# Eleven projections of the last layer's chunks: one f32 product in four passes, or three products of rounded parts

## The reference, cut to what matters

```python
xn = rmsnorm(h) * g_sio                      # h: layer norm of x, scaled and shifted
z  = sigmoid(xn @ w_ln_z.T + b_ln_z)         # in logs in the reference
dt = xn @ w_dt.T + b_dt
h_t = sigmoid(-dt) * h_{t-1} + z * sigmoid(dt)     # a scan over each sequence
y  = (h_t @ w_y.T + b_y) * silu(xn @ w_yact.T + b_yact)
x1 = h + y
xn2 = rmsnorm(x1) * g_ffn
hid = (xn2 @ w_fc.T + b_fc) * silu(xn2 @ w_fcact.T + b_fcact)   # 128 -> 512 features
x2 = x1 + hid @ w_out.T + b_out
# then x = x + gate * x2, a layer norm, and a channel mix: three 128x128 products
```

## Time and profile before

| | us |
|---|---|
| median of three runs (lowest to highest) | 768.26 (766.97 to 769.05) |
| the profiled execution | 762.66 |
| its span, first to last instruction | 760.9 |
| TensorE busy in the span | 696.3 |
| VectorE, ScalarE, GpSimd busy | 505.9, 481.8, 388.6 |

### The profile page before, as it was taken

One profiled execution on the slowest core, in us unless ns is written; L12 is line 12 of the kernel. 1 busy time (PEld: TensorE's weight loads), 2 busy tenths in 40 slices (PEclk: granted clock), 3 DMA queues, 4 the chain that ended last, 5 costly groups with the idle time before them and its releaser, 6 DMA issues.

```text
span 760.9 us, 12350 instructions
## 1 busy us (share of the span) xinstructions
PE 696.3 (92%) x3608; PEld 424.0 (56%) x3608; DVE 505.9 (66%) x1906; ACT 481.8 (63%) x734; POOL 388.6 (51%) x562
## 2 busy tenths in 40 slices
PE   4999999999997999887999699996999999999994
PEld 4544444545444544347988699984655544444442
DVE  2598879989998899973452244422345678795572
ACT  2767687677784767565544355552587959777553
POOL 7427354656776667742422255534455575722253
PEclk9999999999999999998999899999899999999998
DMA  9992000000000000028676688811010101000002
GB/s 273 380 383 70 1 1 0 9 15 15 19 19 16 14 15 22 22 84 236 193 203 206 192 249 245 243 51 32 28 29 24 33 23 40 25 4 0 0 15 83
DMA packets 65597, 66.79 MB, mean 88 GB/s; under 512 B 7105, under 2 KB 48410, under 8 KB 65530
## 3 DMA queue, kind: packets, MB, share of 16 engines
q1 hardware_dynamic: 59152, 52.46, 22.8%
q0 software_dynamic: 6320, 13.53, 5.6%
q10 hardware_dynamic: 58, 0.02, 0.0%
HBM read 37.80 MB, written 28.18 MB: 87 GB/s over the span
## 4 chain that ended last, share of the span: by engine, by line
PE 56%; DVE 22%; issue 7%; ACT 5%; DMA 4%; SPq 2%; POOL 2%; DVEq 0%; ACTq 0%; POOLq 0%
PE PS L1085 9%; DVE JK L1271 8%; PE PS L948 4%; PE PS L1135 3%; PE PS L891 3%; PE PS L986 3%; PE PS L1066 3%; PE PS L1149 3%; PE PS L1142 3%; PE PS L897 2%; PE PS L903 2%; PE PS L988 2%; PE PS L911 1%; DMA got<-expert_out,IG 1%; PE PS L1072 1%
## 5 line engine op out<-in xcount | busy, mean ns | idle before, releaser
L1271 DVE CUSTOM_DVE_ANT_0 JK<-PS,CM 128x256 bf16<-128x256 f32 (+1 forms) x512 | 149.1, 351 | 7.0 <-PE PS L948 5.7
L1763 ACT ACTIVATE GF<-PS,XN 128x256 f32<-128x256 f32 x156 | 73.5, 475 | 72.9 <-PE PS L1074 41.6
L948 PE MATMUL PS<-KZ,QS 128*128 128x512 f32 x192 | 88.4, 497 | 7.8 <-DVE MX L1271 5.6
L1085 PE MATMUL PS<-WD,GF 128*128 128x128 f32 x624 | 94.0, 276 | 0.0
L1941 POOL DMA_INDIRECT got<-expert_out,IG x64 | 64.5, 1007 | 50.3 <-DMA got<-expert_out,IG 33.1
L1085 PEld LDWEIGHTS PS<-WD,GF 128*128 128x128 f32 x624 | 86.4, 193 | 2.8
L1913 POOL DMA_INDIRECT expert_rows<-five,IU x64 | 63.3, 990 | 32.5 <-DMA expert_rows<-five,IU 14.9
L1724 ACT ACTIVATE PA<-PS 128x1024 f32<-128x1024 f32 x64 | 64.7, 1026 | 15.2 <-PE PS L971 14.1
L1863 POOL TENSOR_SCALAR H<-xc,MOD 128x256 f32<-128x256 f32 x56 | 33.3, 603 | 68.0 <-DVE xc L1240 60.8
L1900 POOL TENSOR_SCALAR_AFFINE_SELECT PA<-PA 128x256 f32<-128x256 f32 x128 | 49.8, 419 | 27.9 <-ACT PA L1724 27.3
L1924 POOL DMA_DIRECT2D expert_out<-YT x39 | 21.7, 558 | 80.3 <-DVE YT L1523 80.3
(11 more groups left out here) (289 smaller groups left out, 1710.1 us busy)
## 6 DMA issues: line engine op xcount, KB each, us to landing
expert_rows<-five SPq DMA_DIRECT2D x16, 1024.0 KB, 12.6
WU<-in_L_ffn_up_w SPq DMA_DIRECT2D x39, 256.0 KB, 3.2
WD<-in_L_ffn_down_w SPq DMA_DIRECT2D x39, 256.0 KB, 3.4
XT<-expert_rows SPq DMA_DIRECT2D x39, 128.0 KB, 3.7
expert_out<-YT POOLq DMA_DIRECT2D x39, 128.0 KB, 3.4
BD<-in_L_ffn_down_b SPq DMA_DIRECT2D x39, 64.0 KB, 3.3
PA<-in_L_attn_x SPq DMA_DIRECT2D x8, 256.0 KB, 5.5
out<-yo SPq DMA_DIRECT2D x8, 256.0 KB, 2.4
```

The lines of the kernel that those rows point to most:

```text
L948: pe.matmul(bk.rearrange("p (j n) -> p j n", n=wd), q, ks, start=True, stop=True).then_inc(sems["mx_mm"], 1)
L1085: m = pe.matmul(bk[:, b], g[:, b], wd[:, k, :], start=(k == 0 and t == 0), stop=(k == 3 and t == blocks - 1))
L1271: m = dve.tensor_tensor_reduce(JK[n % 2][:, s], bk[:, s], CM[:, 256 - wd:256] if wd == 128 else CM[:, 0:256], -1.0, 3.0e38, ALU.add, ALU.m ...
L1763: act.activation(GF[slot["gf", kind, u, k]][:, 0:n], bank("up", kind, u, k)[:, 0:n], ACT.Gelu, bias=bias).then_inc(sems["gelu"], 1)
```

## The change

The 88 products of normed rows are made from rounded parts. `rmsnorm` for the norms "g" and "h" now writes its f32 result over the reciprocal roots (the `rs` buffers) instead of XN; a new ACT stage `xhi` copies it to a float32r tile `xh`, a new POOL stage `xlo` writes the difference to `xl` (three pairs of such tiles); each product becomes three float32r matmuls, high weight by high rows, low weight by high rows and high weight by low rows. `zd` does the four matmuls with high rows first and then waits for the low ones. The weights' parts are made once in the experts' stage by three new DVE subtractions (`twl`). The product of low by low is not computed.

Around it: the first sigmoid factor A goes to XN instead of a ring of its own; the output copies have two buffers instead of three, `rr` two instead of three; the weights are turned in five groups instead of six. `ORDER2` is written anew, `ORDER1` gets the three `twl` steps. Two entries in `NARROW`, the table of how long TensorE is really active in a stage, change what `arrange` believes of attention, so that it places fillers at new points: 17 groups of fillers instead of 7, mostly of one matmul. Gathers wait for each other as before.

```diff
+PARTS = (0, 2, 3)
...
-NARROW = {"dpm": 0.06, "rtm": 0.05, "vm": 0.15, "modmm": 0.2}
+NARROW = {"dpm": 0.06, "rtm": 0.05, "vm": 0.15, "modmm": 0.2, "atm": 0.11, "mxm": 0.213}
...
-LANDS = {"gather": 2.5, "scatter": 2.5, "fetch": 3.0}
+LANDS = {"gather": 2.5, "scatter": 2.5, "fetch": 3.0, "store": 2.0}
...
-    "APAPAAAAAAAAAPAPAPAPACACACACAAAAAAAAAAAAAAAAAEAEAEAEAAAAAAAAAAAAAAAAAGAGAGAAAAAPAXAXAXAAAAADAPAPABAAAIAPAGAIAPAPAPAPAAAA"
...
+    "APAPAPAAAAAAAPACACAAAAAAAAAAAEAEACACAAAAAAAAAAAAAAAAAEAEAXAXAXAAAAAAAAABAPAPAPAGAGAGAGAAAPAPAAAPAPAPAPAPAPAIAAAAAAAAAAAP"
...
-        yield stage("rms_rs", c, s, takes=[(RS_, "rrs", (c, s), ("xn", c, s))])
+        yield stage("rms_rs", c, s, takes=[(RS_, "rrs", (c, s), ("xn" if s == "q" else "xl", c, s))])
         yield stage("rms_norm", c, s, after=[("vecs",)])
+        if s != "q":
+            yield stage("xhi", c, s, takes=[(XP, "xp", (c, s), ("ya_mm", c) if s == "g" else ("f_mm", c, 3))])
+            yield stage("xlo", c, s)
 
...
-        for n in range(6):
-            yield stage("tw", n, takes=[(RR, "tw", (n,), ("tw_hi", n))], after=[("up", "s", NS - 1, 3), ("load_late",)])
+        for n in range(5):
+            yield stage("tw", n, takes=[(RR, "tw", (n,), ("tw_lo" if n in PARTS else "tw_hi", n))], after=[("up", "s", NS - 1, 3), ("load_late",)])
+            if n in PARTS:
+                yield stage("twl", n)
...
-        yield stage("rec", c, takes=[(SZ, "sz", (c,), ("Bz", c)), (SD, "sd", (c,), ("Bz", c)), (AA, "A", (c,), ("hs", c))])
+        yield stage("rec", c, takes=[(SZ, "sz", (c,), ("Bz", c)), (SD, "sd", (c,), ("Bz", c))])
...
-        yield stage("yam", c, takes=[(BK, "ya_bk", (c,), ("ya", c))], after=[("rms_norm", c, "g")])
+        yield stage("yam", c, takes=[(BK, "ya_bk", (c,), ("ya", c))], after=[("zd", c)])
...
-        yield stage("fam", c, k, takes=[(BK, "fa_bk", (c, k), ("fa", c, k))], after=[("rms_norm", c, "h")])
+        yield stage("fam", c, k, takes=[(BK, "fa_bk", (c, k), ("fa", c, k))], after=[("xhi", c, "h"), ("xlo", c, "h")])
-        yield stage("fm", c, k, takes=[(BK, "f_bk", (c, k), ("hf", c, k))])
+        yield stage("fm", c, k, takes=[(BK, "f_bk", (c, k), ("hf", c, k))], after=[("fm", c, k - 1)] if k else [])
...
-        yield stage("yo", c, takes=[(YO, "yo", (c,), ("yo", c))])
+        yield stage("yo", c, takes=[(YO, "yo", (c,), ("store", c))])
...
-TURN = ((0, 2), (2, 4), (6, 1), (7, 4), (11, 4), (15, 4))
-NAMES = ["L1_attn_w_ln_z", "L1_attn_w_dt", "L1_attn_w_y", "L1_attn_w_yact", "L1_ffn_W_r", "L1_ffn_W_k", "L1_ffn_W_v"]
+TURN = ((0, 3), (3, 4), (7, 4), (11, 4), (15, 4))
+NAMES = ["L1_attn_w_ln_z", "L1_attn_w_dt", "L1_attn_w_yact", "L1_attn_w_y", "L1_ffn_W_r", "L1_ffn_W_k", "L1_ffn_W_v"]
...
-    WL = sb("WL", [128, 19, 128])
+    WL, WLH, WLO = sb("WL", [128, 8, 128]), sb("WLH", [128, 11, 128], R), sb("WLO", [128, 11, 128], R)
...
+    xh, xl = ([sb(f"{n}{k}", [128, CH], R) for k in range(3)] for n in ("xh", "xl"))
...
+    def parts(k):
+        k = k if k < 3 else k - 4
+        return WLH[:, k, :], WLO[:, k, :]
...
-            pe.matmul(bank("z", c), wl["L1_attn_w_ln_z"], chunk(XN, c), start=True, stop=True).then_inc(sems["z_mm"], 1)
-            for e in prior["d", c]:
-                w.wait_ge(*at(*e))
-            pe.matmul(bank("d", c), wl["L1_attn_w_dt"], chunk(XN, c), start=True, stop=True).then_inc(sems["d_mm"], 1)
+            high, low = rounded(c, "g")
+            w.wait_ge(*at("xh", c, "g"))
+            w.wait_ge(*at("tw_lo", 0))
+            for use, k in (("z", 0), ("d", 1)):
+                for e in prior[use, c]:
+                    w.wait_ge(*at(*e))
+                pe.matmul(bank(use, c), parts(k)[0], high, start=True, stop=False)
+                pe.matmul(bank(use, c), parts(k)[1], high, start=False, stop=False)
+            w.wait_ge(*at("xl", c, "g"))
+            pe.matmul(bank("z", c), parts(0)[0], low, start=False, stop=True).then_inc(sems["z_mm"], 1)
+            pe.matmul(bank("d", c), parts(1)[0], low, start=False, stop=True).then_inc(sems["d_mm"], 1)
 
...
+            pe.matmul(bank("fa_bk", c, k), parts(11 + k)[0], high, start=True, stop=False)
+            pe.matmul(bank("fa_bk", c, k), parts(11 + k)[1], high, start=False, stop=False)
+            pe.matmul(bank("fa_bk", c, k), parts(11 + k)[0], low, start=False, stop=True).then_inc(sems["fa_mm"], 1)
...
-            if s == "h":
-                w.wait_ge(*at("ya_mm", c))
-            dve.scalar_tensor_tensor(two(chunk(XN, c)), hc(c), weight, two(rs_of("rrs", c, s)), ALU.mult, ALU.mult
-                                     ).then_inc(sems["xn"], 1)
+            o = chunk(XN, c) if s == "q" else rs_of("rrs", c, s)
+        def twl(n):
+            k0, kn = TURN[n]
+            o = k0 if k0 < 3 else k0 - 4
+            w.wait_ge(*at("tw_hi", n))
+            dve.tensor_tensor(WLO[:, o:o + kn, :].rearrange("p k d -> p (k d)"), bank("tw", n)[:, 0:128 * kn],
+                              WLH[:, o:o + kn, :].rearrange("p k d -> p (k d)").bitcast(F), ALU.subtract).then_inc(sems["tw_lo"], 1)
...
-            A, Bv = aa[slot["A", c]], bz[slot["Bz", c]]
+            A, Bv = chunk(XN, c), bz[slot["Bz", c]]
...
+        def xhi(c, s):
+            w.wait_ge(*at("xn", c, s))
+            for e in prior["xp", c, s]:
+                w.wait_ge(*at(*e))
+            act.activation(rounded(c, s)[0], rs_of("rrs", c, s), ACT.Copy).then_inc(sems["xh"], 1)
...
+        def xlo_(c, s):
+            high, low = rounded(c, s)
+            w.wait_ge(*at("xh", c, s))
+            pool.tensor_tensor(low, rs_of("rrs", c, s), high.bitcast(F), ALU.subtract).then_inc(sems["xl"], 1)
```

120 lines of the change are left out of this document (64 added, 56 removed), and 5 rows, old and new, of tables (HELD, SIGNALS).

## The result

The changed kernel takes 778.59 us (median of four, 772.06 to 782.07) beside 768.65 for the kernel before: a ratio of 1.0101, with a 95% interval from 1.0058 to 1.0145. With two later batches of runs it was timed 22 times, with a median of 777.0; the kernel before, timed beside every batch of later runs, 92 times, with 768.2. So it is slower by about 1.1%, where 763.3 and faster had been forecast, with a range of 754 to 771. The 92 runs of before lie between 761.4 and 774.9 us, 1.8% and not the 0.3% of the first three. A ratio takes only runs within 1.5% of the fastest of their kernel; medians are over all runs.

The account below looks back on a forecast made before the run. Gathers and VectorE, together with TensorE, bound the last layer until chunk 7's `fin2` (673.9 us), TensorE's work after it. Terms -6.0 + 0 + 0 + 1.0 + 0 = -5.0 us took the median from 768.26 to 763.3, range 754 to 771.

Parts of the forecast that it names:

- The price of a pass: TensorE's 88 changed products: 0.23 us per single pass, three cost 0.69 instead of 0.86, so each saves 0.17.
- what it saves behind the hinge: From chunk 7's `fin2` to the end: TensorE's remaining work falls from 74.5 to 68.5 us, saving 6.0.
- the hinge: Start of chunk 7's `fin2`, 673.9 us: gathers and VectorE decide ahead of it together with TensorE, TensorE's remaining work behind it.
- Ahead of the hinge 0: First to last `fin2`: POOL's delay of gathers and VectorE's earlier results cancel; 0, with ends of -3 and +7 us.
- The latency added: 0, up to 3.8: Copy and subtraction after each RMS norm, 1.9 us, twice per chunk: hidden by TensorE work; for chunk 7, 0 to 3.8.
- The stores, +1.0: Last output copies, with two buffers, wait for the store of two copies before: +1.0 us, ends 0 and 2.6.
- Before 510 us ... I take 0: Stages ahead of the last layer: three DVE subtractions and ten fillers of 0.2 us cost 0, at most 2 us.
- The slower case: Rival: `xlo` before a gather waits for `xhi`; gathers 7.4 us late, chunk 7's norms add 3.8; 774.5 us, chance 0.15.
- POOL taking it back: Rival: six shared gaps between gathers lengthen by 0.9 each, gather 7 and the hinge 5 us later; 768.3 us, chance 0.16.
- Full pace: Rival: TensorE sets the pace throughout, gathers not held up, all 10.5 us arrive, less 1.0 for stores; 758.8 us, chance 0.22.

Follow-up runs that it names:

- d: The kernel before with only its last layer's written order replaced by the changed kernel's, without roundings and subtractions, four passes kept: 770.1 us, ratio 1.0030.
- g: The changed kernel with its 88 products in one four-pass instruction each, all conversions and orders kept: 784.1 us, ratio 1.0204.
- e: The changed kernel without row roundings and subtractions: VectorE's normalisation writes rounded rows, the third pass rereads high rows: 767.9 us, ratio 0.9997.

## Why the prediction was wrong, step by step

**The price of a pass, and what it saves behind the hinge: right.** Pieces of 0.23 stand in the chain behind the last `fin2`, and that stretch shrank by 4.8 us where 5.0 had been said. That the sum fits so well was luck in part: 6.0 less for TensorE and 1.0 more for stores had been said, and it is 4.8 less and nothing more. Of the 6.0, three products moved ahead of the hinge were 2.6 (3 x 0.86); the new order alone gave 1.6 (`d`). The passes were the other 3.4 and gave 3.1 (`g` to after).

**"Ahead of the hinge 0": the step that failed in the layer.** The hinge came 7.0 us later in the layer, the upper end. Two things were left out of its sum, one was mis-sized. Passes were taken to save nothing there, since the gathers hold the hinge; they save 5.8 (`g`: 154.3, after: 148.5), or 7.4 with no conversions in the way (`d` to `e`), since the gathers themselves come 4 to 5 us earlier. The new order was taken as free; it costs 7.4 (`d`), nearly all of it behind the last gather, where the sum had `cmb` follow the gather in 2.85 us as before and VectorE's queue now holds it for 5.0. The conversions were given 0 to 7.4 and settled at 0 with VectorE's earlier results against them; they cost 7.0 up to the hinge (148.5 to 141.5, `e`), 3.1 of it `xlo` and 3.9 the rounding on ScalarE.

**"The latency added: 0, up to 3.8": mis-sized.** It had been priced for chunk 7 alone, with other chunks' products as cover. The cover is no help to the queues: GpSimd waits 23.9 us at `xl` for ScalarE, with gathers behind it. For the layer the order is +5.8, the passes -11.5 (`d` to `e`) and the conversions +7.9, in all +2.2. That these add up is no check, since each is the step from one kernel to the next; taken through `g` instead they are +5.8, -8.9 and +5.3.

**The stores, +1.0: wrong and small.** The last copy waits for TensorE; in the earlier trace rows a copy had waited for a store, and here none of the last four does:

```profile
766.75 0.60 ACT L1858 ACTIVATE yo<-PS 128x512 f32<-128x512 f32 x1 [0.70 <-PE PS L1206]
```

**"Before 510 us ... I take 0": the step with the largest error.** In the profiles 12.2 of the 14.4 us stand here. Of the +5.1 from the first load to the first `fin2`, 3.1 are the three subtractions by their place, where the text had VectorE's load in mind and not its queue, and about 2 go with one more fall of the clock. Of the +7.1 to the first load, at least 3.2 arise at one place with the new fillers (five of 0.4 us in attention, not ten of 0.2), which were taken as 2 us at most; the rest is open, as the granted clock up to there was the same. Over all runs the changed kernel's mean clock is 0.0067 lower, which at 4.3 us per 0.01 is 2.9 us. At equal clock it is 6.9 us slower, of which the layer's 2.2 and the subtractions' 3.1 make 5.3, and 1.1 go with the fillers (6.9 less 5.8). What part of the 2.9 the fillers cause is open.

**The rivals.** The slower case named the mechanism (`xlo` waiting for `xhi` in front of a gather) and its sign, with 774.5 us, but it had 0.15. POOL taking it back, 0.16, had gather 7 land 5 us later and the hinge by as much; it is issued 2.9 later and the hinge comes 7.0 later. Full pace, 0.22, was right about the passes (11.5 without the conversions, 10.5 forecast). Slower and full pace were not alternatives: both came, one against the other. No rival had the order or the stage ahead of 510 us as a price.

## What to carry to other kernels

When a cheaper product needs converted inputs, price the conversion by the queue that it waits in and what stands behind it there, not by its duration or by the load of its engine: 16 roundings and 16 subtractions that other work was to hide cost 7.9 us of the 11.5 that the passes gave. A one-off preparation belongs where its input has long been there and its engine idles next; three subtractions cost some 3 us of their stretch in one place and none about 40 us later. And an order written for one set of stages has a price when it is rewritten: run the old kernel in the new order before the rest, and look at what now stands ahead of the instruction that the next stage waits for. Fillers are no free change either: compare the time between two instructions that both kernels have.

## What the runs showed of the hardware

- The time of one kernel went with its mean granted clock, 4.3 us for 0.01; the kernel before ranged from 0.958 to 0.983, and the whole change is no larger than two such steps of 0.01. With five more filler products TensorE's clock fell between 151 and 158 us in all nine profiles, and in none of eleven without them; the passage around it took 28.1 us or more in place of 24.9.
- A single-pass product between others of its kind took 394 ns in its group with 0.23 us of the chain; the first of three, which often stands behind an f32 product, had 493 to 665 in its group.
- Rounding a row of 128x512 took 0.63 us on ScalarE, the subtraction 1.28 on GpSimd and 0.69 on VectorE; rounding the weights from SBUF on VectorE 0.42 to 0.49.
